# One projection and two copies change their places in a software-pipelined attention loop

## The reference

```
q = rope((layernorm(x) @ Wq).reshape(b, n, 32, 8), pos)
k, v = split(ctx @ Wkv, 2);  k = rope(k, ctx_pos)
logits = einsum('bqhd,bkhd->bhqk', q, k) * scale
w = softmax(logits, axis=-1)
attn = einsum('bhqk,bkhd->bqhd', w, v)
x = x + attn @ Wout + bout
x = x + moe(layernorm(x))
```

## Time and profile before

| what | value |
|---|---|
| median of 3 runs | 370.2 us (369.3, 370.2, 370.22) |
| profiled execution, its own time | 369.8 us |
| its span, first to last instruction | 367.8 us |
| mean granted TensorE clock | 0.956 |
| PE busy | 315.5 us (86%) |
| PE weight loads busy | 218.1 us (59%) |
| DVE busy | 221.8 us (60%) |
| ACT busy | 188.2 us (51%) |
| POOL busy | 196.3 us (53%) |

### The profile page before, as it was taken

The page is one execution under the profiler, slowest core; times in us unless marked ns, Lnnn a source line. Parts: engine busy times, 40 slices in busy tenths (PEclk is TensorE's granted clock), DMA queues, the critical chain, the costliest instruction groups (busy, mean ns, idle before and its releaser), DMA issues. The chain is left out here.

```text
span 367.8 us, 9525 instructions
## 1 busy us (share of the span) xinstructions
PE 315.5 (86%) x3094; PEld 218.1 (59%) x3094; DVE 221.8 (60%) x621; ACT 188.2 (51%) x389; POOL 196.3 (53%) x285
## 2 busy tenths in 40 slices
PE   0668999999999999999998558889999989999930
PEld 0445777777777777777676324445765764555520
DVE  4466777676777666777777445788549044454520
ACT  4153668767668767668667375271344342233310
POOL 5569876667866667866200181053788411525460
PEclk9996999999999999999999858999999999999985
DMA  6511114454454454543210033203123275953446
GB/s 169 183 37 30 31 25 116 119 149 118 136 138 115 116 148 115 146 132 87 77 46 3 0 115 111 69 0 87 46 84 105 67 219 181 295 136 44 52 50 228
DMA packets 33292, 37.93 MB, mean 103 GB/s; under 512 B 7808, under 2 KB 27568, under 8 KB 33200
## 3 DMA queue, kind: packets, MB, share of 16 engines
q1 hardware_dynamic: 22610, 22.03, 20.6%
q10 hardware_dynamic: 8030, 11.93, 11.7%
q0 software_dynamic: 2624, 3.61, 5.9%
HBM read 26.36 MB, written 8.96 MB: 96 GB/s over the span
## 5 line engine op out<-in xcount | busy, mean ns | idle before, releaser
L405 ACT ACTIVATE pw<-bank 128x512 f32<-128x512 f32 x128 | 78.0, 615 | 53.3 <-PE bank L635 45.1
L496 DVE TENSOR_REDUCE mx<-bank 128x4 f16<-128x512 f32 x128 | 86.2, 684 | 9.6 <-PE bank L611 8.2
L624 PE MATMUL bank<-qst,kz 128*128 128x128 f16 x512 | 50.3, 221 | 0.3 <-ACT pw L405 0.2
L611 PE MATMUL bank<-kz,qst 128*128 128x512 f16 x128 | 49.6, 389 | 0.9 <-DMA kz<-kT 0.9
L624 PEld LDWEIGHTS bank<-qst,kz 128*128 128x128 f16 x512 | 36.0, 98 | 14.6 <-issue 6.8
L943 POOL DMA_INDIRECT acc<-ac,dst x16 | 23.5, 1471 | 35.3 <-ACT ac L1025 23.4
L264 POOL TENSOR_TENSOR t<-qk,RC 128x512 f32<-128x512 f32 x15 | 19.1, 1272 | 40.2 <-ACT qk L416 40.2
L503 DVE COPY mxs<-bank 8x128 f16<-8x128 f16 x64 | 13.4, 210 | 36.4 <-PE bank L615 36.4
L635 PE MATMUL bank<-pw,V 128*32 128x128 f32 x1024 | 34.6, 276 | 0.0
L1245 PE MATMUL mbank<-hT,WSG 128*128 128x512 f16 (+1 forms) x144 | 32.0, 379 | 0.0
L635 PEld LDWEIGHTS bank<-pw,V 128*32 128x32 f32 x1024 | 26.0, 109 | 7.3 <-issue 5.0
(11 more groups left out here) (192 smaller groups left out, 640.2 us busy)
## 6 DMA issues: line engine op xcount, KB each, us to landing
ring_gu<-in_L_ffn_w_gate_up ACTq DMA_DIRECT2D x20, 352.0 KB
kz<-kT SPq DMA_DIRECT2D x64, 64.0 KB, 2.0
ring_dn<-in_L_ffn_w_down ACTq DMA_DIRECT2D x10, 352.0 KB
ring_gu<-in_L_ffn_w_gate_up SPq DMA_DIRECT2D x8, 352.0 KB
X<-in_x SPq DMA_DIRECT2D x4, 512.0 KB, 8.1
table<-ac SPq DMA_DIRECT2D x8, 256.0 KB, 2.2
acc<-X SPq DMA_DIRECT2D x4, 512.0 KB, 3.7
out<-acc SPq DMA_DIRECT2D x4, 512.0 KB, 5.6
```

What stands on the lines that cost most here:

```text
L405: act.activation(pw[g % 4][:, :], STB[g % 2][:, :], ACT.Exp, scale=SCALE).then_inc(exp_ok, 1)
L496: dve.tensor_reduce(mx[u // 2 % 2][:, u % 2:8:2], SB[u % 2][:, :].rearrange("p (j t) -> p j t", j=4), axis=AX.X, op=ALU.max, negate=True). ...
L611: pe.matmul(SB[u % 2][:, :], qst[m.par][:, u, :], kz[m.par][:, :, u, :], start=True, stop=True).then_inc(s_mm, 1)
L624: ins = pe.matmul(STB[g % 2][:, j * P:j * P + P], kz[m.par][:, j, g, :], qst[m.par][:, g, :], start=True, stop=True)
```

## The change

On PE, the output projection of step 7 moves from the end of the step to between the logits and the maxima transpose. Also on PE, in step 0, the value products of b-1 go ahead of the input transposes of b+3. On ACT, in step 0, the copy of the values of b+1 goes ahead of the exponential of quad 0. No instruction of work is added or taken away.

```diff
             def period(b):                       # scalar engine
                 for g in range(QUADS):
-                    if inside(b):
-                        act.wait_ge(st_mm, QUADS * b.n + g + 1)
-                        at_least(act, pv_mm, QUADS * b.n + g - 3)
-                        act.activation(pw[g % 4][:, :], STB[g % 2][:, :], ACT.Exp, scale=SCALE).then_inc(exp_ok, 1)
                     if g == 0 and inside(m1):
                         at_least(act, v_mm, m1.n + 1)
                         act.wait_ge(consts, 6)
                         at_least(act, pv_mm, QUADS * b.n)
                         act.copy(Vh[m1.par][:, :, :, 0:HD], M0[:, 0:D].rearrange(...)).then_inc(v_ok, 1)
+                    if inside(b):
+                        act.wait_ge(st_mm, QUADS * b.n + g + 1)
+                        at_least(act, pv_mm, QUADS * b.n + g - 3)
+                        act.activation(pw[g % 4][:, :], STB[g % 2][:, :], ACT.Exp, scale=SCALE).then_inc(exp_ok, 1)
                     if g == 0 and inside(m3):
                         evac_xcT(m3)
...
             def period(b):                       # tensor engine
                 for g in range(QUADS):
                     if inside(b):
                         logits_k(b, g)
+                    if g == 7 and inside(o):
+                        project_out(o)
                     if g % 2 == 1:
...
                     if g == 0 and inside(m1):
                         project_v(m1)
-                    if g == 0 and inside(m3):
-                        transpose_xc(m3)
                     if g == 0 and inside(o):
                         for q in range(4, QUADS):
                             weigh_values(o, q)
+                    if g == 0 and inside(m3):
+                        transpose_xc(m3)
...
                     if g == 6 and inside(m2):
                         transpose_k(m2)
-                    if g == 7 and inside(o):
-                        project_out(o)
```

## The result

The change makes the kernel slower: 372.85 us, the median of 22 runs, against 369.81 us for 22 runs of the kernel before; the ratio is 1.0075, with a 95% interval of 1.0053 to 1.0097. The forecast was 369.9 with a range up to 371.9. The profiled execution took 372.47 us (span 370.7, granted clock 0.952), against 369.8, 367.8 and 0.956.

A forecast was written before the change was run, and what follows sets the result against it. The prediction took PE's order and its few waits as the bound. Regular periods -1.6, last two full periods +0.4 and first batch +0.9 gave -0.3 us against the profiled 369.8, or 369.5; forecast median 369.9, range 368.4 to 371.9.

The forecast's parts named there:

- What bounds the kernel: Regular periods of 11.03 us: only PE's order and its few waits count; L589's wait put on ACT's copy, not POOL.
- Step 7: Output projection ahead of the maxima transpose: fills PE's 0.28 us wait for DVE; logits to value projection 1.89, gain 0.22 a period.
- The term that I had put at nothing: SP's queue after step 7: second half's maxima about 0.5 us later, kz loads behind them, not wanted before step 3; cost 0.
- Step 0: Earlier value products and copy end L589's wait, but the exponential delays the input evacuation and key projection; 0.09 us lost a period.
- the 0.09: Key projection L578 in regular periods: starts 3.12 us behind the value projection instead of 3.03; loss 0.09, bounds 0 and 0.2.
- the forecast's -1.6: Twelve regular periods, batches 1 to 12, each -0.22 + 0.09 = -0.13 us.
- the prediction's own sign of being wrong: Prediction wrong if the period is under 10.85 or over 10.97 us, or the first batch's key projection isn't late.
- The last full periods: Batches 13 and 14, without inputs to transpose: ACT's later chain loses 0.44 us, output projection's move gains 0.22; together +0.4.
- The first batch: ACT's exponential table load moves from idle time to behind the copy of values; key projection 36.61 instead of 35.74, loss +0.87 us.
- this rival: First batch's table load costs more, as by the drain; worked out as a second 1.30 us load: 371.2 us, chance 0.08.
- Faster: Key projection not late at all, so a regular period gives its whole 0.22 us; 368.9, or 368.4; chance 0.24.
- Slower: First half's maxima arrive too late for L624 of step 0; output projection's move gives nothing in 14 periods; 373.1 us, chance 0.15.

The follow-up runs named there:

- Step 0 alone: Kernel before with only the two moves of step 0, on PE and ACT, the output projection where it was; 372.56 us, ratio 1.0116.
- the second trace: The changed kernel run again without any edit, for another trace; 375.3 us over 4 runs, ratio 1.0112 to the kernel before.
- load in step 2 and exponential first: Changed kernel with ACT's exponential ahead of the copy again and the first expert-weight load issued in step 2, not 1; 369.74 us, ratio 0.9983.

## Why the prediction was wrong

**What bounds the kernel: right.** PE's order and its few waits. The wait at L589 was ACT's, not POOL's: with the earlier copy L589 starts at 2.41 instead of 2.59, and POOL was left as it was.

**Step 7: the mechanism right, the rest of the queue missed.** In undisturbed periods L655 starts 0.22 behind the logits and L601 1.89 (140.65 to 142.54), as forecast. The step that failed is the sentence "The second half's maxima are issued about 0.5 later, and on SP the four kz loads stand behind them. They are not wanted before step 3, so I take nothing." The 0.5 was right (0.43), the nothing was not. I followed the queue to the kz loads, asked who wants these, and stopped. Behind them stands one thing more, the third transfer of maxima, wanted in step 4. It could be issued up to 0.45 us later than before at no cost (3.15, with one DMA added), and in the even periods 4 to 10 it went 0.55 to 0.66 later. To the delay of the second transfer came the jump of SP's loop, which the profile does not count as busy and which came out of its cover (with SP written out, the changed kernel gains 1.7 us by its ratio), and the weight load on ACT's queue, beside which the transfer now fell. The term that I had put at nothing is the main miss: in the even periods 4 to 10, +2.0 us in place of -0.5.

**Step 0: right in kind, the 0.09 wrong in sign.** The copy starts at 1.67, not 1.75, and the evacuation of the inputs ends at 2.92, not 2.98. The key projection follows it by 0.05, not by 0.14, and starts at 2.97 instead of 3.12, earlier than before and not later. So an undisturbed period is shorter by 0.24 (11.03 to 10.79) and not by 0.13. Of the forecast's -1.6, -1.0 did come, in the five odd periods 3 to 11; that five periods gave most of what twelve were to give is luck. By the prediction's own sign of being wrong, a period under 10.85 or over 10.97, both kinds of period fail, the odd ones mostly by being too short and the even ones by being too long. Step 0 alone showed that its own gain is taken by the wait for DVE, so it exists only together with step 7.

**The last full periods: one right, one not.** The forecast was +0.22 for each of periods 13 and 14. Period 13 has +0.26. Period 14 has -0.17, from first logits to first logits: the queries come as late as in 13, but step 7 gives more there, since L615 had waited 0.56 us for DVE ahead of the change (at 193.97). Period 12, which the forecast took as a regular one, has +0.18 instead of -0.13: its logits of step 6 start at 8.50 instead of 8.20. A load of expert weights (L156) is issued at 5.31 there and the fourth transfer of maxima at 5.60, the same meeting as with the weight load in step 2; that it is the cause is argued from this likeness.

**The first batch: right.** Forecast +0.87, measured +0.82 in period 0. The load takes 1.28 us, and from its start to that of the exponential are 1.29 us; it starts 0.02 behind the end of the copy. The Trainium skill, ScalarE: Activation LUTs, section What ACT_TABLE_LOAD costs, counts some 1380 ns of drain beside the 1283 ns of the load. The load agrees; the drain has no room here either, so this rival falls.

**The rivals.** "Faster" (chance 0.24) had the right mechanism for step 0: the key projection isn't late, and an undisturbed period gives its whole 0.22. "Slower" (chance 0.15) had the right number, 373.1, and half of the right mechanism: a transfer of maxima that comes too late for its logits. But it named step 0 and the first half's maxima. There L624 waits a little in some periods (0.41 on the weight-load side at 131.29), which makes the way from the logits of step 7 to L601 up to 0.22 us longer than 1.89. The decisive place is step 4, so that the number came out is luck. The condition there can be read from the periods 3 to 11 of all fourteen traces, 126 in number. In 24 of them the third transfer is issued between 0.05 us ahead of the weight load and 0.38 behind it, and in all 24 the logits of step 4 are late, at 6.14 to 6.72. In the other 102 it is issued at least 0.25 ahead of the load, or the load is in step 2, and the logits start at 5.59 to 5.86. Between 0.25 and 0.05 no run has a value.

**Sum.** Forecast -0.3. Measured between first and last L601 +4.2 in the first trace: first batch +0.8; odd periods 3 to 11 -1.0; even periods 4 to 10 +2.0; period 12 +0.2; period 13 +0.3; periods 1 and 2 +1.9. Of these last, 1.6 are the score product of period 2 that waits for a late kz load, and about 0.4 the logits of step 4 in period 1; why both transfers were late is open. In the second trace the sum is +2.5.

## What to carry to other kernels

When an instruction is delayed on a DMA-issuing queue, walk down that queue to the first wait that truly absorbs the delay, and for every transfer passed on the way compare its arrival with its reader; the one that you know of is rarely the last. Count what the profile leaves out on that queue, loop jumps above all, which are free only as long as a wait behind them is long enough to hold them. And look at what other queues issue at the same moment: a small transfer that a reader waits for should be issued ahead of a large one that nobody is waiting for.

## What the hardware showed that was not expected

- An 8-row transfer of maxima (2 KB) was there within 2.1 us of its issue where no weight load was near (3.51 to 5.61, load in step 2 and exponential first), and within 2.6 where the weight load of 352 KB went 0.25 behind it. When it went beside or behind that load, its reader started 2.8 to 3.3 us behind its issue (123.58 to 126.47; 82.52 to 85.53), though the two are issued by different engines.
- One jump of SP's loop costs about 0.36 us (0.48 between two issues against 0.12), in either kernel. While it was covered, taking it away gave nothing (ratio 0.9986). Uncovered, all of them cost 1.7 and 5.8 us by the ratios of two pairs of kernels, 4.2 and 2.7 by their traces.
- All 20 of SP's 1570 issues that took over 0.7 us (up to 1.86, instead of 0.51 to 0.68) stand within 0.5 us of a packet of an instruction queue. It is a coincidence in every trace, and no experiment.
